# A scratch tensor of query and key parts, grouped by eight heads in DRAM

## What is computed

```python
scores = einsum('bhqd,bhkd->bhqk', q, k)
rel_q = einsum('bhld,lrd->bhlr', q, pos_emb)
rel_k = einsum('bhrd,lrd->bhlr', k, pos_emb)
scores = (scores + rel_q + rel_k) / sqrt(D)
probs = softmax(scores)
ctx = einsum('bhqk,bhkd->bhqd', probs, v)
out = layernorm(ctx_all_heads @ Wo + bo + xn)       # attention
y = sum over the two picked experts of weight * (silu(n2 @ w1 + b1) @ w2 + b2)
```

## Time and profile before

| | |
|---|---|
| median of three runs | 1890.74 us (1885.74 to 1891.82) |
| profiled execution | 1886.8 us, its span 1885.2 us |
| PE busy | 1579.0 us, 84% |
| VectorE busy | 1252.6 us, 66% |
| ACT busy | 1041.5 us, 55% |
| GpSimd busy | 577.4 us, 31% |
| read from and written to DRAM | 435.11 and 195.82 MB |

### The profile page before, as it was taken

How to read it: one execution, slowest core, us unless ns; L and a number is a source line. 1 busy time by engine, 2 the same in 40 slices (tenths; PEclk the granted TensorE clock), 3 DMA queues, 4 the chain that set the end, 5 groups by cost and what they waited for, 6 DMA issues and landing times.

```text
span 1885.2 us, 35485 instructions
## 1 busy us (share of the span) xinstructions
PE 1579.0 (84%) x12086; PEld 1182.2 (63%) x12086; DVE 1252.6 (66%) x3122; ACT 1041.5 (55%) x2242; POOL 577.4 (31%) x760
## 2 busy tenths in 40 slices
PE   5758640385999988998999899989999999999996
PEld 3324330385888978887888788955555555555553
DVE  6746545360557555655565566768988888997895
ACT  2425320122655534554445355379888888987883
POOL 1352337351010001010111000115263555635546
PEclk9878665698999989999999899999999999999998
DMA  6563426778799889889998988799989999999991
GB/s 212 175 188 113 138 95 217 205 182 277 219 333 331 265 275 371 293 296 347 387 365 280 351 297 296 300 314 317 337 256 332 296 292 324 280 343 283 289 318 46
DMA packets 227284, 510.58 MB, mean 271 GB/s; under 512 B 38208, under 2 KB 84800, under 8 KB 222624
## 3 DMA queue, kind: packets, MB, share of 16 engines
q1 hardware_dynamic: 202144, 410.57, 67.8%
q0 software_dynamic: 23808, 93.54, 14.4%
q10 hardware_dynamic: 1152, 4.19, 0.6%
HBM read 435.11 MB, written 195.82 MB: 335 GB/s over the span
## 4 chain that ended last, share of the span: by engine, by line
PE 45%; DMA 9%; DVE 9%; issue 8%; SPq 4%; ACT 3%; POOL 3%; POOLq 0%; DVEq 0%; ACTq 0%
PE up L1071 9%; PE dn L1083 9%; PE rl L1051 9%; PE pt L1467 7%; DMA scratch_rel<-rel_out 6%; PE sc L1459 4%; PE cx L1480 3%; DVE rel_out L999 3%; SPq L885 2%; DVE probsT L1352 2%; DMA rows<-scratch_sorted 1%; PE wo_ps L1502 1%; DMA late_by_head<-scratch_parts 1%; DVE square L1010 1%; SPq L890 1%
## 5 line engine op out<-in xcount | busy, mean ns | idle before, releaser
L999 DVE TENSOR_TENSOR rel_out<-rl,square 128x1024 f32<-128x1024 f32 x256 | 402.0, 1572 | 271.3 <-PE rl L1051 187.5
L976 ACT COPY square<-rl 128x1024 f32<-128x1024 f32 x256 | 259.2, 1015 | 334.2 <-DVE rel_out L999 226.3
L1309 ACT ACTIVATE square<-square,row_least 128x512 f32<-128x512 f32 x512 | 365.6, 717 | 38.0 <-DVE row_least L1344 37.8
L1344 DVE CUSTOM_DVE_ANT_1 square<-sc,square 128x512 f32<-128x512 f32 x512 | 337.8, 686 | 60.2 <-issue 55.3
L1467 PE MATMUL pt<-ident,square 128*128 128x128 f32 x2048 | 323.0, 281 | 29.2 <-ACT probsT L1316 23.7
L1071 PE MATMUL up<-rowsT,w_b 128*128 128x128 f32 x2272 | 317.1, 287 | 15.9 <-issue 8.0
L1467 PEld LDWEIGHTS pt<-ident,square 128*128 128x128 f32 x2048 | 249.3, 145 | 112.8 <-DVE probsT L1352 42.5
L1083 PE MATMUL dn<-w_b,hid 128*128 128x256 f32 x1136 | 299.5, 393 | 0.0
L1071 PEld LDWEIGHTS up<-rowsT,w_b 128*128 128x128 f32 x2272 | 283.7, 198 | 18.3 <-issue 10.7
L985 ACT ACTIVATE hid<-up,w_b 128x128 f32<-128x128 f32 x568 | 162.2, 372 | 126.4 <-PE up L1071 126.4
L1459 PE MATMUL sc<-late_by_head 96*128 96x512 bf16 x512 | 203.5, 398 | 12.7 <-DVE row_least L1344 10.5
(11 more groups left out here) (197 smaller groups left out, 1690.4 us busy)
## 6 DMA issues: line engine op xcount, KB each, us to landing
scratch_rel<-rel_out SPq DMA_DIRECT2D x256, 512.0 KB, 4.6
square<-scratch_rel SPq DMA_DIRECT2D x256, 512.0 KB, 8.5
w_b<-in_w POOLq DMA_DIRECT2D x71, 1152.0 KB
w_b<-in_w POOLq DMA_DIRECT2D x71, 1028.0 KB
krows_sb<-scratch_stack SPq DMA_DIRECT2D x768, 64.0 KB, 3.4
late_by_head<-scratch_parts SPq DMA_DIRECT2D x384, 64.0 KB, 6.3
scratch_parts<-part SPq DMA_DIRECT2D x96, 128.0 KB
qrows_sb<-scratch_stack SPq DMA_DIRECT2D x192, 64.0 KB, 3.1
```

Of the source, the lines that this page charges most:

```text
L976: nc.scalar.copy(dst, src).then_inc(s_kc, 1)
L999: nc.vector.tensor_tensor(out[n % SRING][:], rl[r][:].rearrange("p a (b s) -> p (a b) s", s=TILE), square(tile)[:, u * UN:(u + 1) * UN], A ...
L1309: nc.scalar.activation(sm[j][:, i], sm[j][:, i], ACT.Exp, bias=least[:, j, i:i + 1], scale=-1.0, accum_out=es[:, g // 2 % 2, i, 2 * j + g ...
L1344: nc.vector.tensor_tensor_reduce(sm[j][:, i].rearrange("p (c s) -> p c s", c=LT), sc[i % 2][:].rearrange("p (c s) -> p c s", c=LT), rq[j][ ...
```

## The change

`parts` gets the shape (16, 6, 16, 8, 512): group of eight heads, part, dimension, head in the group, position. The eight heads of one dimension are 8 KB in sequence, the next dimension follows at once, and what one store writes is one piece of 128 KB. `GH` is 8. Everything that touches the tensor is written for this shape: the stores of the projection, the loads of both turnings, which are now two for each batch (one for each group of eight heads) and so count twice 16 in the semaphore that ACT and VectorE wait for, and `load_qk`, whose four heads are half of a group.

```diff
@@ -39,6 +39,7 @@
 LAST_REL = 68
 REPACKS = (2, 1, 2, 1, 2)
 
+GH = 8
 PAIRS = [(0, 0), (0, 1), (0, 2), (1, 0), (1, 1), (2, 0)]
 KS = D * len(PAIRS)
 WIN = 2 * S
@@ -191,7 +192,7 @@
                     sp.wait_ge(done, 4 * (b + 1) if k == 0 else b + 1)
                     for c in range(4):
                         at = b * H + (c % 2) * (H // KC)
-                        dst = t["parts"][c // 2 * PARTS + k, :, at:at + H // KC].rearrange("d h s -> h d s")
+                        dst = t["parts"][at // GH, c // 2 * PARTS + k].rearrange("d h s -> h d s")
                         sp.dma_start(dst, part[b % PRING][k][:, c]).then_inc(s_ps[b % PRING], 16)
                 if b + 2 < B:
                     store_xn(b + 2)
@@ -463,8 +464,9 @@
             for b in range(B):
                 if b >= 2:
                     repack_done(sp, b - 2)
-                src = t["parts"].rearrange("q d h s -> (q d) h s")[:, b * H:(b + 1) * H, 0:2 * TILE]
-                sp.dma_start(by_head[b % 2][:], src).then_inc(s_bh[b % 2], 16)
+                for i in range(H // GH):
+                    src = t["parts"][b * H // GH + i].rearrange("q d h s -> (q d) h s")[:, :, 0:2 * TILE]
+                    sp.dma_start(by_head[b % 2][:, i * GH:(i + 1) * GH], src).then_inc(s_bh[b % 2], 16)
             for b in range(B - 2, B):
                 repack_done(sp, b)
             for i in range(2):
@@ -536,7 +538,7 @@
                 nc.scalar.activation(pr[:], pr[:], ACT.Exp).then_inc(s_ex, 1)
 
             def repack(b):
-                act.wait_ge(s_bh[b % 2], 16 * (b // 2 + 1))
+                act.wait_ge(s_bh[b % 2], 16 * (H // GH) * (b // 2 + 1))
                 nc.scalar.copy(*repacked(b)).then_inc(s_ba, 1)
 
             take_v(0)
@@ -650,7 +652,7 @@
                 nc.vector.tensor_copy(slots[:, :, own], slot_f[:]).then_inc(s_slot, 1)
 
             def repack(b):
-                dve.wait_ge(s_bh[b % 2], 16 * (b // 2 + 1))
+                dve.wait_ge(s_bh[b % 2], 16 * (H // GH) * (b // 2 + 1))
                 nc.vector.tensor_copy(*repacked(b)).then_inc(s_bd, 1)
 
             def finish():
@@ -891,8 +893,9 @@
 
             for b in range(B):
                 after(sp, s_br, b - 1)
-                src = t["parts"].rearrange("q d h s -> (q d) h s")[:, b * H:(b + 1) * H, 2 * TILE:4 * TILE]
-                sp.dma_start(by_head[b % 2][:], src).then_inc(s_bh[b % 2], 16)
+                for i in range(H // GH):
+                    src = t["parts"][b * H // GH + i].rearrange("q d h s -> (q d) h s")[:, :, 2 * TILE:4 * TILE]
+                    sp.dma_start(by_head[b % 2][:, i * GH:(i + 1) * GH], src).then_inc(s_bh[b % 2], 16)
             for x in range(KRING):
                 load_k(x)
             for p in range(PIECES):
@@ -1165,7 +1168,7 @@
                 after(sp, s_sc, (g - 1) * HG * ST)
                 for dst, side in ((qs, 0), (ks, 1)):
                     for n, pair in enumerate(PAIRS):
-                        src = t["parts"][side * PARTS + pair[side], :, g * HG:(g + 1) * HG]
+                        src = t["parts"][g * HG // GH, side * PARTS + pair[side], :, g * HG % GH:g * HG % GH + HG]
                         sp.dma_start(dst[i][n * D:(n + 1) * D], src).then_inc(s_qk[i], 16)
 
             load_qk(0)
@@ -1631,7 +1634,7 @@
         v = np.ascontiguousarray(v)
         ins[f"in_{name}"] = v
         t[name] = nc.dram_tensor(f"in_{name}", v.shape, mybir.dt.from_np(v.dtype), kind="ExternalInput").ap()
-    for name, shape, dt in (("parts", (2 * PARTS, D, BH, S), BF16), ("stack", (LT, 2 * PARTS, D, TILE, BH), BF16),
+    for name, shape, dt in (("parts", (BH // GH, 2 * PARTS, D, GH, S), BF16), ("stack", (LT, 2 * PARTS, D, TILE, BH), BF16),
                             ("xn", (B * S, E), F32), ("va", (B * S, E), F32), ("x1", (B * S, E), F32),
                             ("sorted", (ROWS, E), F32), ("ysorted", (NBLK * TB, E), F32),
                             ("rel", (BH, PITCH), F32)):
```

## The result

The changed kernel took 1899.4 us in the median of 20 runs (1890.2 to 1909.3), the kernel before 1890.8 us in 20 runs (1881.5 to 1896.7). The ratio is 1.0053, with a 95% interval of 1.0037 to 1.0068: slower by some 9 us. No change was forecast (1891.0 us). The profiled execution of the changed kernel took 1908.6 us with a span of 1907.0, a long one among its runs (9 us above their median), so its span isn't to be set against 1885.2 as it stands; what counts is where it differs in kind.

What follows compares the result with a forecast made beforehand. Attention was taken as paced by TensorE and its feeding engines, with little DMA room. Terms 0 + 0 + 0.3 + 0 = +0.3 us on the profiled 1886.8 gave 1887.1, placed at the runs' median as 1891.0; range 1880 to 1897 us.

Steps and rivals of the forecast that it cites:

- stores and attention loads: Projection's stores and attention's loads of `parts`: 0 us each, bounds -1.2 us for stores, 0 and -7.3 for loads.
- the control at 32 KB: Attention loads from `stack`, rows 32 KB apart: 177 GB/s backlogged against 168 for `parts` at 128 KB, so distance isn't the reason.
- VectorE's stops in attention: Four waits of 3 to 4.4 us ahead of a score; forecast to stay 3 us or more if right.
- faster rival: Attention and experts' start: distance slows loads at 32 and 128 KB, not at 8; -8.6 us, 1882.4 us; chance 0.29.
- the slower one: End of projection: neighbouring packets hinder the last 24 stores, a third longer, +5.7 us, 1896.7 us; chance 0.15.
- route's sixteen loads: Route: eight repack loads become sixteen, nobody's wait names them; 0 us, or 0.3 us per extra issue without cover.
- the step on the repack loads at the start of the experts: Experts' start: eight repack loads become sixteen, eight extra issues of 0.305 us; +0.3 us, bounds -1.3 and +2.4.
- the 3.93 us ahead of the third copy: Experts' start: VectorE's wait for a 10.66 us load ending at 370.94; gain of 1.3 us there if distance were to blame.
- the cover: Experts' start: all extra issues but the last batch's are hidden by the copies, 4.8 us each, that SP waits for.

Runs made afterwards that it cites:

- e12: Kernel before, with only attention's loads taken from the new layout's addresses (permuted values): ratio 1.0001 to the kernel before.
- e14: Kernel before, with only the projection's stores sent to the new layout's addresses (permuted values): ratio 1.0011 to the kernel before.
- a0: The changed kernel run again unaltered for a second profile: ratio 1.0038 to the kernel before.
- e15: Kernel before, with the turning loads of route and the experts' start cut in two and taken from the new addresses: ratio 1.0041 to the kernel before.
- e16: Kernel before, with only the turning loads at the experts' start cut in two and taken from the new addresses: ratio 1.0036 to the kernel before.
- e1: Kernel before, old layout, with the turning loads of route and the experts' start cut in two by eight heads: ratio 0.9985 to the kernel before.
- e11: Changed kernel, with ScalarE's queue issuing the second load of the first two batches: ratio 1.0032, again 1.0034, to the kernel before.
- e7: Kernel before, old layout, with the late loads of the first two batches cut in four: ratio 1.0037 to the kernel before.

## Why the prediction was wrong

**Right: the distance of the rows doesn't set the time of a packet.** I took 0 for stores and attention loads, from the control at 32 KB. 352 GB/s for 351, 159 for 168 (beside another queue), and e12 and e14 at 1.0001 and 1.0011, bear it out. VectorE's stops in attention are smaller in this profile than the four of before (two of 3 us, the others 1.3 to 2.3), but the stage took as long. The faster rival (8.6 us, chance 0.29) is refuted, and so is the slower one as I told it: the last stores didn't get in each other's way, and the next stage started 2.1 us later in this profile (127.27, here 129.36) but at 127.10 us in a0.

**Right: route's sixteen loads.** No wait names them, and e15 isn't told apart from e16.

**Wrong: the step on the repack loads at the start of the experts, +0.3 us with bounds of -1.3 and +2.4.** It was the right place and the only term with a cost, but it was priced as SP's time, eight issues of 0.305 us, and at another wait: I looked at the 3.93 us ahead of the third copy, and put the wait ahead of the second at nothing. Two things failed. First, the price of an issue was read from loads that each stood by themselves and had another form; in the new layout it is 542 to 639 ns (and right behind another load some 530 even in the old one, in e1). Second, and this is the step that failed in mechanism, I asked how long SP takes and not what the later load runs into. The rows of before had the answer beside them: the chain's own 10.66 us for a load of that kind, where such a load alone takes 3.4 us by my own estimate from the earlier trace rows, says that something shares the engines with it. For the fourth load it was the weights. A load that starts 0.4 us later in that race isn't 0.4 us late but 10: 11.1 us to landing in e1, 21.1 in the changed kernel. What the step should have held is a new stop of 8.5 to 9.0 us, with the `stack` store 7.7 to 9.9 us later in the three profiles. How much of the 8.6 us between the medians is this stop stays open, as said above.

**Wrong too: the cover.** I wrote that all extra issues but the last are covered by the copies that SP waits for. That holds from the third batch on. For the first two, SP waits for nothing, and they are the ones in the race.

**The chances.** Slower got 0.15 and only by way of the stores. A case "the second load of a batch meets the weights, VectorE's queue stops, the price is a stop of the order of the earlier trace rows's 3.9 us and more" was to be had from the same rows and was missing. The range ended at 1897 us; the time was 1899.4.

## What to carry to other kernels

When a load is cut in two, or its issue gets longer, look at what else starts in the same microseconds: here, where big packets of another queue followed close behind, the last pieces of the small ones landed later by far more than the delay of their issue. Price such a change at the wait that it can create, with all that stands behind that wait on the engine's queue, and not at the time of the issue. And look where the waits are tight by tenths of a microsecond rather than where the bytes are: all the traffic of attention was indifferent to this change, the four loads at the start of the experts were not. And test the repair too: e11 took the stop away and still read 1.0032.

## What the runs showed of the hardware

- Two queues with a backlog on the same DMA engines were served packet for packet: 194 to 218 small ones of 512 B beside 196 to 217 weight packets of about 7 KB in 4 us, in the changed kernel, e7 and e16, and within three of each other in each quarter of a microsecond in the changed kernel. The queue with the small packets moved 0.10 to 0.11 MB and the other 1.39 to 1.46.
- A load of the same bytes (384 or 768 KB) took SP 304 ns at least to issue where heads and dimensions have different strides, and 542 ns where they follow in one even stride (8 KB or 16 KB between dimensions). At 9 KB it was 304 ns again.
- Rows to neighbouring partitions 8, 32 or 128 KB apart made no difference that can be told: 159 (beside another queue), 177 and 168 GB/s backlogged for loads to 16 partitions, and 352 and 351 for the stores of 1 KB pieces at 8 and 128 KB.
